# Moving the transposes of the next cross queries between the two halves of the cross values in a two-layer decoder kernel

## What is computed

```
x = layernorm(x + L1_attn(x))      # 16 heads of 16 channels, causal, 64 tokens
x = layernorm(x + L1_xattn(x, c))  # 32 heads of 8 channels, no mask

def L1_xattn(x, context, Wq, Wk, Wv):
    q, k, v = heads of x @ Wq.T, context @ Wk.T, context @ Wv.T
    q, k = rmsnorm(q), rmsnorm(k)                    # over 8 channels
    attn = softmax(q @ k.T * 8 ** -0.5)
    return attn @ v
x = layernorm(x + L1_ffn(x))       # 8 experts, the best 2 of each token
```

## Time and profile before

| | |
|---|---|
| median of 3 runs | 1157.33 us (1155.63 to 1158.86) |
| the profiled execution: its own time | 1160.24 us |
| its span | 1158.4 us |
| TensorE matmuls busy | 1070.5 us, 92% of the span |
| VectorE busy | 496.1 us, 43% |
| ScalarE busy | 502.9 us, 43% |
| GpSimd busy | 442.4 us, 38% |
| mean granted TensorE clock | 0.979 |

### The profile page before, as it was taken

How to read it: one execution, slowest core, us unless ns; L and a number is a source line. 1 busy time by engine, 2 the same in 40 slices (tenths; PEclk the granted TensorE clock), 3 DMA queues, 4 the chain that set the end, 5 groups by cost and what they waited for, 6 DMA issues and landing times. The chain is left out here.

```text
span 1158.4 us, 29034 instructions
## 1 busy us (share of the span) xinstructions
PE 1070.5 (92%) x10270; PEld 833.3 (72%) x10271; DVE 496.1 (43%) x1339; ACT 502.9 (43%) x1303; POOL 442.4 (38%) x565
## 2 busy tenths in 40 slices
PE   8888989889799999999988999997879999999997
PEld 4466666656455677777756778775568899999997
DVE  2365655655483133333345666667346400000513
ACT  2444455445333333333434666664343343333342
POOL 2023131211147886877736664324523000200534
PEclk9999999999989999999998999999989999999999
DMA  6189559031094465565463110000176555655663
GB/s 208 42 305 361 195 174 345 2 102 56 1 329 125 160 195 159 159 193 150 126 264 124 43 48 21 20 20 29 46 264 214 175 157 177 213 178 164 219 215 102
DMA packets 119339, 176.09 MB, mean 152 GB/s; under 512 B 17440, under 2 KB 96912, under 8 KB 117776
## 3 DMA queue, kind: packets, MB, share of 16 engines
q1 hardware_dynamic: 93328, 131.86, 35.2%
q0 software_dynamic: 9696, 26.75, 7.3%
q10 hardware_dynamic: 16208, 15.96, 4.1%
HBM read 105.07 MB, written 68.16 MB: 150 GB/s over the span
## 5 line engine op out<-in xcount | busy, mean ns | idle before, releaser
L2883 PE MATMUL bank<-m_XGT,m_w 128*128 128x128 f32 x1248 | 148.1, 278 | 0.0
L2883 PEld LDWEIGHTS bank<-m_XGT,m_w 128*128 128x128 f32 x1248 | 145.2, 195 | 0.2
L2897 PE MATMUL bank<-w,m_HT 128*128 x624 | 141.0, 379 | 0.0
L2897 PEld LDWEIGHTS bank<-w,m_HT 128*128 128x128 f32 x624 | 115.7, 190 | 14.1
L2727 ACT ACTIVATE m_HT<-bank,m_b 128x128 f32<-128x128 f32 x312 | 89.2, 369 | 76.6 <-PE bank L2883 76.6
L1798 PE MATMUL bank<-m_W,m_XGT 128*128 x316 | 107.6, 463 | 0.4 <-issue 0.3
L2691 POOL DMA_INDIRECT m_GA<-ys,r_pos x32 | 31.8, 994 | 138.7 <-SPq L2642 129.7
L1655 ACT ACTIVATE m_XGT<-bank 128x256 f32<-128x256 f32 x79 | 30.3, 384 | 117.1 <-DVE m_US L1742 116.7
L1734 DVE TENSOR_TENSOR m_H<-bank,m_SG 128x176 f32<-128x176 f32 x79 | 27.0, 341 | 118.6 <-ACT m_SG L1659 118.6
L1412 POOL DMA_INDIRECT GA<-ys,r_pos x64 | 64.7, 1011 | 31.2 <-issue 20.5
L1592 POOL DMA_INDIRECT xs<-X,r_pos x64 | 63.2, 988 | 27.8 <-issue 14.6
(11 more groups left out here) (441 smaller groups left out, 2274.4 us busy)
## 6 DMA issues: line engine op xcount, KB each, us to landing
m_w<-in_m_w SPq DMA_DIRECT2D x35, 1024.0 KB, 5.3
xs<-zeros SPq DMA_DIRECT2D x1, 10112.0 KB, 34.5
ys<-zeros SPq DMA_DIRECT2D x1, 10112.0 KB, 34.2
ys<-m_US ACTq DMA_DIRECT2D x79, 128.0 KB
m_GS<-xs SPq DMA_DIRECT2D x72, 128.0 KB
w<-in_m_w SPq DMA_DIRECT2D x8, 1024.0 KB, 13.9
xs<-zeros SPq DMA_DIRECT2D x1, 6400.0 KB, 23.0
ys<-zeros SPq DMA_DIRECT2D x1, 6400.0 KB, 40.7
```

The costliest lines, as they stand in the source:

```text
L2883: last = nc.tensor.matmul(BU[i][:, c * P:(c + 1) * P], w1[:, b, m, lo:lo + P], XGT[:, b % 2, m * P:(m + 1) * P], start=m == 0, stop=m == K ...
L2897: last = nc.tensor.matmul(BY[b % 2][:, 0:DIM], HT[:, b % 2, c, :], w2[:, bass.ds(e, 1), c, :], start=c == 0, stop=c == CH - 1)
```

## The change

In the seven rounds where both pairs i and j exist (i from 1 to 7), the wait for `ln_done[1]` and the turn `xb_xtr` leave the end of the round and go ahead of the second tile's 32 heads of cross values. In round 0, where there are no cross values, they stay where they were. No instruction is added or removed, and nothing changes on the other engines.

```
                                 pe.wait_ge(lo_done.sem, lo_done.at(i, t))
                             else:
                                 pe.wait_ge(xo_done.sem, xo_done.at(j - 1, t))
+                            if has(i) and t == 1:
+                                pe.wait_ge(ln_done[1].sem, ln_done[1].at(i, 1))
+                                turn_pair(("xb_xtr", i), X[:, pair_tiles(i), :])
                             for h in range(H32):
                                 m, r, c = h // 16, h % 16 // 4, h % 4
                                 n, a = divmod(h, 2)
...
                             last.then_inc(xo_full.sem, 1)
-                    if has(i):
+                    if has(i) and not has(j):
                         pe.wait_ge(ln_done[1].sem, ln_done[1].at(i, 1))
                         turn_pair(("xb_xtr", i), X[:, pair_tiles(i), :])
```

## The result

The changed kernel takes 1162.82 us, median of 11 runs (1158.01 to 1164.25), against 1157.95 us for the kernel before beside it (11 runs, 1155.63 to 1162.49). The ratio is 1.0036, interval 1.0023 to 1.0049: 4.2 us slower, from 2.6 to 5.7 (the two medians alone differ by 4.9). The profiled execution took 1164.07 us around a span of 1162.2 us, where the one before had 1158.4: 3.8 us more.

What follows compares the result with a forecast made beforehand. TensorE was taken to bound the steady rounds, VectorE's chains rounds 7 and 8. Costs of 0.26 (round 1), 1.36 (rounds 2 to 5), 0.77 and 0.77 sum to 3.2 us on 1157.33: 1160.5 us, range 1157.3 to 1162.8.

Steps and rivals of the forecast that it cites:

- No wait to remove in rounds 1 to 5: Before the cross queries, ScalarE's copy of the turned rows is already hidden; gain taken as zero, at most 0.08 us a round.
- The cut costs 0.34: Rounds 2 to 5: a turn inside the cross-value stream takes 0.77 us instead of 0.43 at the round's end, net 0.34 each.
- Round 1, 0.26: Stream already cut by a wait for ScalarE; norm done about 0.1 us after the second tile could begin; net cost 0.26 us.
- Round 6 even: Round 6 into 7, TensorE alone: first cross-value load to cross queries 5.19 us against 5.22 before, so no net change.
- Rounds 7 and 8, 0.77 each: VectorE's gapless chains start 0.77 us later behind the delayed second tile, and TensorE waits for them: 0.77 us lost in each.
- (a): Clock rival: TensorE's longer wait in round 7 prolongs the half-clock stretch, up to 1.5 us more, 1162.0 us; chance 0.15.
- (b): Rival: VectorE's late chains in rounds 7 and 8 have slack, leaving only the cut stream's 1.6 us, 1158.9 us; chance 0.10.
- (c): Rival: the 0.42 us before the cross queries is really a wait for ScalarE's copy; -1.4 us, 1155.9 us; chance 0.10.
- TensorE's wait of 1.98 us in round 7: Sign to look for in the changed profile: this wait behind VectorE grows from 1.98 to some 2.75 us.

## Why the prediction came out as it did

The direction and the size were right. The forecast was 3.2 us; the places in the trace give 3.23; the runs give 4.2 with an interval of 2.6 to 5.7. The median, 1162.82, lies at the upper edge of my range, and I had put more weight on "same" (0.56) than on "slower" (0.40).

- *No wait to remove in rounds 1 to 5.* Shown: the distance from masks to cross queries stayed at 0.53 with the copy 2.4 us early, and a copy made later on purpose is hidden for 0.16 us. What stands there comes with the change of shape behind the masks, 0.42 us with no copy to wait for. I had the slack 0.06 too long, because I had taken the 0.05 us of round 7, where the load itself waits, for every wait.
- *The cut costs 0.34.* It measured 0.29 in rounds 4 and 5 (twice that with two cuts); the first load behind a tile comes 2.00 to 2.01 us after the tile's start, not 2.03, which is 0.15 to 0.16 for the switch instead of 0.18, and with both tiles the whole is 0.05 less. Rounds 2 and 3 had 0.36 because the norm was late there, by 0.07, which I had ruled out: I had allowed no more than 0.05 us from the norm's end to the turn, as from ScalarE's copy, and it is 0.22 to 0.23.
- *Round 1, 0.26.* It measured 0.42, by the same error: waiting for the norm cost 0.27 us, not 0.1.
- *Round 6 even.* It gained 0.08 (2.33 to 2.25 late). The terms came out at 2.00 + 0.59 + 2.01 + 0.53, where I had 2.03, 0.59, 2.03 and 0.54, so at 5.13 us from the first cross-value load to the cross queries instead of 5.19, against 5.22 before.
- *Rounds 7 and 8, 0.77 each.* They measured 0.81 and 0.77 (the 0.81 counts from cross queries that came 0.08 earlier; from the first cross-value load it is 0.72, 8.64 to 9.36). The choice moved away shows for round 7 that VectorE's chain is the cause; for round 8 it rests on the rows. One sign was named wrongly: I expected TensorE's wait of 1.98 us in round 7 to grow. It stayed 1.99, and the lateness showed before the counting matmuls instead, because those too wait for VectorE's choice.

That the sum fits so well is in part luck, for the errors cancel: the cut was cheaper and the norm dearer than I had them. Rounds 1 to 5 came to 1.73 instead of 1.62, the rest to 1.50 instead of 1.54.

Of the rivals, (a) is half there. The granted clock is 0.50 for longer, in this view of the changed kernel (stretch, length, busy times, granted clock), where the kernel before was at 0.50 from 785 to 788:

```profile
788.00:790.00 2.00, 1.33 (x8) 1.09 (x8) 1.97 (x4) 1.11 (x2) 0.75 (x1) 0.73 0.00 0
790.00:794.00 4.00, 3.70 (x17) 2.82 (x16) 2.63 (x6) 2.64 (x5) 2.14 (x4) 0.50 0.00 0
794.00:796.00 2.00, 2.00 (x25) 1.67 (x25) 1.78 (x7) 0.67 (x2) 0.57 (x1) 0.57 0.00 0
```

But the lateness did not grow over it: 3.06 us at the transposes of round 7 and 3.07 (801.33 to 804.40) at its cross values. The slow stretch was taken up by a wait: before the transposes of L2496 TensorE had stood 1.24 us for VectorE, and now it is

```profile
798.35 0.97 PE L2496 MATMUL bank<-ident,GA 128*128 128x128 f32 x4 [0.15 <-DVE GA L2214]
```

Only 0.15 us of that cover is left. What the clock does elsewhere in the runs, and whether it makes up the 1 us between 3.23 and the ratio's 4.2, stays open; the interval holds both. Rivals (b) and (c) are out for the chip of the forecast. On the chips of 1220 us the forecast would have been wrong: the changed kernel's time excludes 3.2 us, though its trace shows the same cost in rounds 4 to 6. Where it is made up there is not shown.

## What to carry to other kernels

A named releaser in front of a wait is only the last event before it. Compare the event's end with the start, and with places where the wait is real: here these lie 0.05 us apart where the load itself waits, 0.11 with one separate waiting instruction in front and 0.22 with two. The steady round's 0.27 us, with one in front, was more than that, and a moved instruction then buys nothing. An instruction set between matmuls of another array shape costs the two switches, here 0.3 us beside its own time, so keep equal shapes together. And ask what starts the longest chain on the other engines: a turn moved ahead of a tile delays that tile's reader, which costs nothing in five rounds, where the reader waits for something later, and everything in two.

## What was not expected of the hardware

The same program took 1158 us on some chips and 1219 to 1220 us on others, with equal durations of many instructions (the indirect transfers' issue, L1412, had a mean of 1011 ns on the one and 1010 on the other). Much of the difference is in standing times between instructions, some [<-issue], some [<-remote]. The mean granted clock was lower too, 0.95 to 0.97 against 0.98 to 0.99. The cause of the standing was not tested.

How soon TensorE follows the event that it waits for depends on how it waits. It started 0.05 us after ScalarE's copy in round 7 before, and 0.05 us after VectorE's norm at 744.02, where the load itself waits. It was 0.11 after the copy in the two kernels with delayed copies, where the trace has one separate waiting instruction in between, and 0.22 after the norm in the moved turn, where it has two. No run varied this alone.
